# Eight block numbers per half step: loaded into VectorE registers without a run-time assertion on each

## The reference

```python
support = x @ weight
msgs = edge_val[:, None] * support[edge_col]
agg = jax.ops.segment_sum(msgs, edge_row, num_segments=N_NODES)
return jax.nn.relu(agg + bias + x)
```

## Time and profile before

| | |
|---|---|
| median of three runs | 3665.72 us (3665.1 to 3668.38) |
| span of the profiled execution | 3248.2 us, mean granted TensorE clock 0.845 |
| median less span | 417.5 us |
| gather, first to last DMA issue | 615.1 to 2707.5 us |
| busy share of the span | PE 79%, POOL 68%, DVE 64%, ACT 39% |

### The profile page before, as it was taken

How to read it: one execution, slowest core, us unless ns; L and a number is a source line. 1 busy time by engine, 2 the same in 40 slices (tenths; PEclk the granted TensorE clock), 3 DMA queues, 4 the chain that set the end, 5 groups by cost and what they waited for, 6 DMA issues and landing times.

```text
span 3248.2 us, 41450 instructions
## 1 busy us (share of the span) xinstructions
PE 2551.2 (79%) x10319; PEld 1953.1 (60%) x10319; DVE 2079.4 (64%) x4779; ACT 1262.1 (39%) x2742; POOL 2193.7 (68%) x2112
## 2 busy tenths in 40 slices
PE   6899989577777686786885876876867874899998
PEld 2788777454544454564654554655645654788887
DVE  7889999455555757657657666566576567566511
ACT  3222221144445434343433443433434441455533
POOL 0466656677777777777777777777777774566644
PEclk9666665598999898897988988988989886899999
DMA  3111112444443543453453453453444448466542
GB/s 114 37 38 32 32 50 78 67 124 118 121 121 112 116 116 119 124 122 116 116 130 117 117 131 117 113 128 115 113 114 111 113 122 278 127 142 145 109 90 44
DMA packets 418592, 353.19 MB, mean 109 GB/s; under 512 B 253830, under 2 KB 359884, under 8 KB 418252
## 3 DMA queue, kind: packets, MB, share of 16 engines
q0 software_dynamic: 106672, 244.73, 28.1%
q1 hardware_dynamic: 303212, 98.01, 13.5%
q10 hardware_dynamic: 8496, 8.09, 0.7%
HBM read 285.06 MB, written 60.91 MB: 107 GB/s over the span
## 4 chain that ended last, share of the span: by engine, by line
PE 30%; DVE 25%; issue 9%; DVEq 8%; POOL 5%; DMA 3%; ACT 1%; POOLq 0%; SPq 0%; ACTq 0%
DVE R L1669 11%; PE ps L1008 9%; DVEq L1660 6%; PE ps L1082 5%; PE ps L1074 5%; PE ps L1198 4%; PE ps L1186 3%; POOL rows L802 2%; DMA out<-y_w,zt 2%; DVEq L1669 2%; POOL out L844 1%; DVE is_low L1656 1%; PE ps L1042 1%; DVE xnT L1729 1%; PE ps L1025 1%
## 5 line engine op out<-in xcount | busy, mean ns | idle before, releaser
L802 POOL DMA_INDIRECT rows<-support,t_dst x1624 | 1579.8, 973 | 512.9 <-issue 457.1
L1008 PE MATMUL ps<-rows,hot 128*128 128x256 f32 x3248 | 907.6, 434 | 378.1 <-DVE R L1669 353.2
L1669 DVE TENSOR_TENSOR R<-R,ps 128x256 f32 x1624 | 682.9, 421 | 717.6 <-PE ps L1008 272.2
L1008 PEld LDWEIGHTS ps<-rows,hot 128*128 128x128 f32 x3248 | 689.2, 220 | 590.6 <-issue 311.1
L1324 ACT ACTIVATE hot<-is_low,t_w 128x128 f32<-128x128 bf16 x1624 | 689.1, 513 | 175.1 <-DVE is_low L1656 159.9
L776 POOL DMA_INDIRECT slots<-rec,st_pos x224 | 315.5, 1409 | 285.1 <-issue 127.7
L949 PE MATMUL ps<-spread,piece 128*104 128x64 bf16 x1568 | 305.1, 369 | 50.6 <-DVE spread L1563 50.6
L949 PEld LDWEIGHTS ps<-spread,piece 128*104 128x104 bf16 x1568 | 303.3, 286 | 60.1 <-issue 29.8
L844 POOL DMA_INDIRECT out<-y_w,zt x112 | 176.9, 1579 | 176.5 <-DVE y_w L1993 90.0
L1198 PE MATMUL ps<-w_all,h_t 128*128 x896 | 206.9, 385 | 1.9 <-DVE y_w L1993 1.9
L1186 PE MATMUL ps<-zt_t,w_sel 128*128 128x256 f32 x896 | 206.3, 384 | 1.8 <-issue 1.0
(11 more groups left out here) (284 smaller groups left out, 2870.6 us busy)
## 6 DMA issues: line engine op xcount, KB each, us to landing
rows<-support,t_dst POOLq DMA_INDIRECT x1624, 2.8
zt<-routed SPq DMA_DIRECT2D x56, 268.0 KB, 2.9
xa<-in_x SPq DMA_DIRECT2D x24, 512.0 KB
w_all<-in_L_ffn_W SPq DMA_DIRECT2D x16, 512.0 KB, 10.3
R<-zeros SPq DMA_DIRECT2D x1, 6400.0 KB, 27.3
xin<-in_x SPq DMA_DIRECT2D x12, 512.0 KB
support<-sup_sb ACTq DMA_DIRECT2D x12, 512.0 KB
xf<-in_x SPq DMA_DIRECT2D x12, 512.0 KB
```

What stands on the lines that cost most here:

```text
L802: pool.indirect_dma_start(out=rows[h][:, j, :], out_offset=None, in_=support, in_offset=bass.IndirectOffsetOnAxis(ap=t_dst[a][:, col:col + ...
L1008: last = pe.matmul(ps[q][:, t * D:(t + 1) * D], lhsT=hot[o][:, q * 2 + t, :], rhs=rows[h][:, q * 2 + t, :], start=True, stop=True)
L1669: dve.tensor_tensor(out=there, in0=there, in1=ps[q][:, t * D:(t + 1) * D], op=ALU.add).then_inc(carried, 1)
```

## The change

The load of the eight block numbers gets an argument that leaves out the check of each value against 0 and `NB` = 49 at run time. The load, its place in the instruction stream, the registers, the additions and all semaphores stay as they are.

```diff
             def carry_on(s):
-                _, where = nc.values_load_multi_w_load_instructions(dest_i[0:1, s * HALF:(s + 1) * HALF], [mybir.EngineType.DVE], min_val=0, max_val=NB)
+                _, where = nc.values_load_multi_w_load_instructions(
+                    dest_i[0:1, s * HALF:(s + 1) * HALF], [mybir.EngineType.DVE], min_val=0, max_val=NB,
+                    skip_runtime_bounds_check_because="a sum over NB rows of flags that are 0 or 1")
                 for q in range(UNITS):
                     for t in range(2):
                         g = s * HALF + q * 2 + t
```

## The result

| | before | after |
|---|---|---|
| median, six runs each | 3662.2 us (3643.28 to 3668.38) | 3604.79 us (3594.46 to 3610.02) |
| ratio, 95% interval | | 0.9847 [0.9819, 0.9874] |
| span of the profiled execution | 3248.2 us | 3592.7 us, its time 3594.46 |

What follows compares the result with a forecast made beforehand. POOL's gathers set the pace; PE and DVE cost time only through a full ring and at the end. 18.0 + 1.4 = 19.4 us off the 3248.2 us span gives 3228.8; with 417.5 carried, 3646.3 us, range 3626 to 3662.

Steps and rivals of the forecast that it cites:

- What the change removes: On line 1660 register operations and assertions go and 203 loads stay, freeing 2.2 us per half step in DVE's sequencer.
- The reading of the two bounds: POOL paces the gather; lateness of PE and DVE costs time only when the ring is full and at the end.
- What POOL gets back, 18.0 us: POOL's waits for PE on line 802 when the four-half-step ring is full, late in the gather, all vanish: 18.0 us.
- The end of the gather, 1.4 us: The last additions on DVE end earlier, limited by PE's last matmuls: 1.4 us gained, between 0 and 2.2.
- The stretching of gathers: POOL's mean gather stays 973 ns despite meeting DVE operations; bounds 956 and 988 ns, -28 to +24 us.
- falling into step: Rival: DVE locks to POOL's 1.25 us beat and collides more with gathers, +66 us, 3713 us; chance 18%.
- The rule named in the prediction: A DVE instruction with two SBUF inputs contends with a GpSimd SBUF reader; whichever comes second is held until the first ends.
- may as well fall on DVE: Collision cost between gathers and DVE operations is paid by whoever comes second, possibly DVE, which has room; no size given.
- The range's lower end: 3626 us for the whole kernel, set for 8 in 10 as two thirds of the way to the stretch bound.
- The third stage shifts as a whole: The stage after the gather has no edit, keeps its 535 us and only starts earlier.
- The median of the runs lies 417.5 us above the span: The timed median's excess over the profiled span holds nothing of the edit and is added unchanged: 417.5 us.
- PE fills the ring by itself: Rival: PE's back-to-back feed-forward matmuls fill the ring, so half the waits stay, 3655 us; chance 8%.

Runs made afterwards that it cites:

- e5: Kernel before, with POOL waiting for PE's sums of three half steps earlier instead of four: 3257.49 us, ratio 1.002.
- e6: Kernel before, with POOL waiting for PE's sums of two half steps earlier instead of four: 3279.01 us, ratio 1.0086.
- e7: Changed kernel, with POOL waiting for PE's sums of two half steps earlier instead of four: 3238.56 us, ratio to before 0.9964.
- e2: Changed kernel as it is, in a series without late PE signals: 3232.57 us, ratio to before 0.9957.
- e1: Kernel before, unchanged, in a series without late PE signals: 3248.29 us, ratio 1.0004.
- e14: Kernel before, unchanged, in a series where PE's semaphore signals arrive late: 3647.82 us, ratio 0.998.
- e13: Changed kernel as it is, in a series where PE's semaphore signals arrive late: 3592.09 us, ratio to before 0.9845.
- e9: Kernel before, with every matmul of line 1008 done twice: 3433.76 us, ratio 1.0574.
- e10: Changed kernel, with every matmul of line 1008 done twice: 3308.19 us, ratio to before 1.0182.
- e11: Kernel before, with one matmul of each pair on line 1008 done twice: 3342.64 us, ratio 1.0288.
- e12: Changed kernel, with one matmul of each pair on line 1008 done twice: 3231.41 us, ratio to before 0.9947.
- e8: Changed kernel as it is, repeated with its profile on a series without late PE signals: 3234.79 us, ratio to before 0.9955.
- e15: Changed kernel with assertions left out on odd half steps only, in a series with late PE signals: 3620.09 us, ratio to before 0.9918.
- e4: Kernel before, with line 1660 standing twice, so each half step has a second load and eight more assertions: 3691.97 us, ratio 1.1367.

## Why the prediction was wrong

Its steps, one by one:

- *What the change removes.* Right: both kinds went with the assertion, the load and the address operations stayed.
- *The reading of the two bounds.* Right for the execution in the profile: POOL paces the gather, PE and DVE cost time only through a full ring. e5 to e7 show the ring's part directly, and the chain passes to POOL in e2.
- *What POOL gets back, 18.0 us.* Right in that condition: 14.5 us in e1, 0.0 in e2. The spans of these two profiled executions differ by 21.2 us: 14.5 from the ring, 5.5 from shorter gathers (1581.2 to 1575.7 us in all), 0.9 from the end. The medians differ by 15.2.
- *The end of the gather, 1.4 us.* In e1 the additions end 6.0 us after POOL's last gather, in e2 5.1 us: 0.9 us.
- *The stretching of gathers.* The mean was 974 ns in e1, 970 in e2 and 973 in the profile of after: no falling into step. With late signals it went from 965 ns (e14) to 976 (e13), 17 us, inside the bounds named. The rule named in the prediction gave a rival that did not come. One reading there is wrong: at the second place of rows 11 the later one is `is_low`, and it takes 0.69 us against a mean of 0.680, so it was not held. Nor was it elsewhere in the trace of before: `is_low` starts inside a gather 157 times and takes 679 ns on average, 681 otherwise, while the 86 gathers that start inside `is_low` take 1180 ns against 945 beside no DVE operation. So nothing here supports the thought that the cost "may as well fall on DVE". (The range's lower end is also 2 us off its own rule: two thirds of 28 us below 3646.3 is 3628.)
- *The third stage shifts as a whole.* Right: 536 us in e1 and in e2.
- *"The median of the runs lies 417.5 us above the span; nothing of the edit is there, so I carry it."* This is the step that failed. Only 1.8 us lie around the span (e1: 3249.59 against 3247.8). The rest is inside the program, nearly all of it in the gather (2490 us in e14 against 2098), as ring waits that the profiled execution did not have. The term that was mis-sized by it is the full ring: 18 us in the profile, 401 us in e14, which is such a run, and 350 still in e13 after the change. The gain is 15 to 17 us in the first kind of execution and 56 to 57 us in the second.

Of the rivals none was this one. "PE fills the ring by itself" came nearest, and I gave it the wrong sign: I took a late PE to leave less to gain, but it leaves more (e9 to e12).

Open: what makes the signals late. One and the same chip has series without them (e5 to e8) and with them (e13 to e15), and before, after and the half show them alike. A low TensorE clock alone does not make them: e4 has 0.82 in its gather, as after has 0.81, and none of its 1107 recorded increments of PE in the gather is late. In the profiles that have them the records are incomplete too: of the 1624 increments that the additions make, 950 are recorded in after, 964 in e13 and 967 in e14, and all in e1, e2 and e4. Whether the recording itself delays the signals, or both have one cause, no run here tells. It was not tried with fewer signals.

## What to carry to other kernels

Set the profiled span against the timed median before anything else: here they differed by 417 us, where span and time of one execution differ by 1.8, and the slack read from the profile was gone in the runs that were timed. Price a change in a consumer at two points, with the ring's cover and with the ring full; here the same 447 us of sequencer work were worth 15 us and 57 us, and up to 126 when PE was late.
## What the runs showed of the hardware that I had not expected

- Doubling the gather's matmuls cost 184 us with the assertions (e9 against before). Without them half as many more cost nothing (e12 stands at 0.9947 of its before, e2 at 0.9957 of its own), and doubling cost 77 us more than that (e10 against e12). None is near the 907 us that their number times their mean says. One reason is the granted clock. In 640 to 2640 us, e1 and then e10:

```profile
640.00:2640.00 2000.00, 1500.81 (x5329) 1065.53 (x5328) 1237.26 (x2794) 852.84 (x1943) 1512.41 (x1554) 0.88 0.47 119
```

```profile
640.00:2640.00 2000.00, 1913.73 (x8184) 1521.93 (x8184) 1197.91 (x2705) 838.21 (x1893) 1464.66 (x1510) 0.99 0.46 116
```

  With PE busy 1914 instead of 1501 us the granted clock was 0.99 instead of 0.88, and the mean of a matmul of line 1008 fell from 437 to 383 ns. Where PE is idle more it is lower: 0.82 in the gather of e4, without late signals, and 0.81 in that of after, with them. How much of the gather's length that accounts for was not separated.
- An added 568 us of sequencer work cost 444 us on a kernel where the removal of 447 us gained 15. This kernel stood just below the point where DVE becomes the pace, and its busy share (DVE 64%) does not say so; busy time and sequencer work together do (1947 of 2098 us of the gather).
